# Second cross attention of a two-layer decoder: scores in half bursts, six turned tiles, the output product in four parts

## The chip, the cores and the metric

The kernel runs on one core of one Trainium2 chip. The metric is the device time of one execution in microseconds. Before the change three runs took 2445.8 us in the median (2442.81 to 2445.98).

## The reference, cut to what matters

A decoder of two layers works on x of 8 batches x 128 rows x 512 columns, with a layer norm ahead of each of six blocks. The change lies in the fifth block, the cross attention of layer 1, and in its join to the sixth, a linear layer with 3-bit weights.

```python
def _L1_xattn_ref(queries, keys, values, Wq, Wk, Wv, Wo):
    EMBED, HEADS, GROUP, KV_HEADS, HEAD_DIM = 512, 32, 4, 8, 16
    q = (queries @ Wq).reshape(b, s, KV_HEADS, GROUP, HEAD_DIM)
    k = (keys @ Wk).reshape(b, s, KV_HEADS, HEAD_DIM)
    v = (values @ Wv).reshape(b, s, KV_HEADS, HEAD_DIM)
    scores = jnp.einsum('bqhgd,bkhd->bhgqk', q, k) * scale
    attn = jax.nn.softmax(scores, axis=-1)
    out = jnp.einsum('bhgqk,bkhd->bqhgd', attn, v).reshape(b, s, EMBED)
    return out @ Wo
x = x + _L1_xattn_ref(_layernorm(x, axis=-1), ctx_4096, ctx_4096, ...)
x = x + _L1_ffn_ref(_layernorm(x, axis=-1), ...)
```

## The kernel before

Everything lies in SBUF; weights come in through five slots. Each weight and activation of the large products is split into a high and a low part, and a product is three matmuls (mm3, L552 to L554). Every engine has its own list of instructions, written out by hand, and semaphores alone join them. The first four blocks fill the first 2200 us; they, and the first layer norm in halves, are not touched.

**The attention of the change.** There are 16 steps n, two for each batch b = n // 2 (its part is n % 2). A step has four groups g of 128 x 512 scores. In a step each group goes through this chain:

- TensorE, `scores(n)` (L991): 8 matmuls on strips of 32 rows of the array, group g on strip g, into the four banks sc0, sc1, pj0 and pj1. One burst fills all four.
- VectorE, `row_max(n, g)` (L2001): the negative row maximum.
- ScalarE, `exps(n, g)` (L1352): four Exp into the tile `probs` of the group, of which there is one for each g.
- VectorE, `row_sums(n, g)` (L2008, L2011): the sum and its reciprocal.
- GpSimd, `normalise(n, g)` (L524): probs times the reciprocal, in place.
- TensorE, `transposes(n, g)` (L1005): four turnings into the bank tp or ou1, in turn.
- ScalarE, `turned_out(n, g)` (L1361): the copy to the tile `turned_whole` (four tiles, one for each g).
- TensorE, `values(n)` (L1019): when all four tiles are there, probs times values into the bank pv.

After a batch's second step ScalarE and VectorE copy pv out as a high and a low part, `heads(b)` (L1367, L2017); TensorE then does `output(b)`, the product with Wo, 12 matmuls into the bank ou0 (L552 to L554); VectorE adds it to x and takes the statistics, `add(b)` (L1429, L2023). The queries of the second half of the batches, `queries(1, c)` for c = 0 to 3 (12 matmuls each into ou0, copied out by ScalarE at L1344), have the place of the first half's queries in `act_whole`, so they wait until steps 5 to 7, when those are used up. VectorE also puts three parts of `dequantise` (L1546 to L1550, the 3-bit weights of the next block) into steps 0, 1 and 3. GpSimd's `block_keys` and `pad_values` (L506, L517) prepare keys and values two steps ahead.

Below, M stands for row_max, E for exps, S for row_sums, N for normalise, T for transposes, U for turned_out, V for values, O for output; "step n" is the pass n of TensorE's loop, "odd" and "even" go by n. In that loop (L1066) TensorE does T(n,0), T(n,1), all of scores(n+1), T(n,2), T(n,3), then in even steps the whole O, then V(n). After step 15 come `turned_weights`, the turned rows of the last layer norm, O(7) and the last block's `product`.

Of the kernel before, what the change touches and what calls it, by code (L numbers as in the profile page):

```python
# [17 lines left out]
FP32 = mybir.dt.float32  # L18
# [7 lines left out]
P = 128  # L26
# [62 lines left out]
KG = 4  # L89
NG = B * KVH // KG  # L90


# [19 lines left out]
def build(nc, a):  # L112
    ctx = ExitStack()
    with ctx:
# [33 lines left out]
        with ExitStack() as shared:  # L148
            TW = shared.enter_context(nc.sbuf_tensor("turned_whole", [P, KG, 512], FP32))
        AL = sb("act_lo", [P, NA], F32R)  # L150
# [397 lines left out]
        def _(pe):  # L548
# [410 lines left out]
            def queries(hf, c):  # L959

                n = hf * KC + c
                bank = ou[0] if hf else query_banks[c]
                if n == 0:
                    pe.wait_ge(x_done, OU["l1x"])
                if n == 2:
                    pe.wait_ge(kr_out, 3)
                if n == 3:
                    pe.wait_ge(q_out, 1)
                if n in (4, 5):
                    pe.wait_ge(x_done, OU["l1x"] + n - 2)  # L970
                if n in (6, 7):
                    pe.wait_ge(q_out, n)
                for k in range(KC):
                    w = both(W, lambda t: wpair(t, WQ_SLOTS, k, 512)[:, c * P:(c + 1) * P])
                    last = mm3(bank[:], w, wide(XT, hf)(k), k == 0, k == KC - 1)
                last.then_inc(q_full, 1)

            def scores(n):

                b, part = n // 2, n % 2  # L980
                pe.wait_ge(kx_ready, n + 1)
                pe.wait_ge(q_out, b // HB * KC + 2 * part + 2)
                if n:
                    pe.wait_ge(lx_exp, n * KG)
                else:
                    pe.wait_ge(pj_done, PJ["ln4"] + B)
                for h in range(2):
                    for g in range(KG):
                        r = slice(32 * g, 32 * g + 32)
                        at = (2 * part + h) * HALF + b % HB * S  # L990
                        last = pe.matmul(score_banks[g][:, h * 256:(h + 1) * 256], AF[r, at:at + S], KX[r, n % 2, :],  # L991
                                         start=True, stop=True)
                        if h:
                            last.then_inc(gs_full, 1)
# [13 lines left out]
            def values(n):  # L1008
# [8 lines left out]
                for g in range(KG):  # L1017
                    at = part * P + 32 * g
                    last = pe.matmul(pv[32 * g:32 * g + 32, :], pads(b)[:, at:at + 32], TW[:, g, :],  # L1019
                                     start=part == 0, stop=part == 1)  # L1020
                last.then_inc(pg_full, 1)

            def output(b):
                pe.wait_ge(on_done, b + 1)
                pe.wait_ge(x_done, OU["l1x"] + b)
                pe.wait_ge(q_out, 4 if b < 2 else 5 if b == 2 else 8)
                if b == 0:
                    ready(4, SLOT["l1x"][4])
                    ready(3, SLOT["l1x_o"])
                for c in range(KC):  # L1030
                    last = mm3(ou[0][:], both(A, lambda t: t[:, ON1 + c * P:ON1 + (c + 1) * P]),
                               wrows(WO_SLOTS)(c), c == 0, c == KC - 1)
                last.then_inc(ou_full, 1)

# [28 lines left out]
            turn(4, range(HB + 2, B))  # L1063
            scores(0)
            queries(0, 3)
            for n in range(NG):  # L1066
# [17 lines left out]
            output(B - 1)  # L1084
            for b in range(B):
# [6 lines left out]
        def _(act):  # L1092
# [244 lines left out]
            def queries(hf, c):  # L1337

                n = hf * KC + c
                act.wait_ge(q_full, n + 1)  # L1340
                if hf:
                    act.wait_ge(gs_full, (7 + c // 2) * KG)
                bank = ou[0] if hf else query_banks[c]
                act.activation(AF[:, c * HALF:(c + 1) * HALF], bank[:], ACT.Copy, scale=HD ** -0.5).then_inc(q_out, 1)  # L1344

# [10 lines left out]
            def turned_out(n, g):  # L1356
                t = n * KG + g
                act.wait_ge(tn_full, t + 1)
                if n:
                    act.wait_ge(pg_full, n)  # L1360
                act.activation(TW[:, g, :], turn_banks[t % 2][:], ACT.Copy).then_inc(tn_out, 1)  # L1361

# [14 lines left out]
            for g in range(1, KG):  # L1377
                exps(0, g)
            for n in range(NG - 1):
# [12 lines left out]
                if n == 6:  # L1392
                    queries(1, 1)
                if n == 7:
                    queries(1, 2)
                    queries(1, 3)
            turned_out(NG - 1, 0)
# [20 lines left out]
        def _(dve):  # L1418
# [607 lines left out]
            for g in range(KG):  # L2026
                row_max(0, g)
            for g in range(KG):
                row_sums(0, g)
            dve.wait_ge(w_hi[3], SLOT["l1x_o"] + 1)  # L2030
            dve.tensor_tensor(WL[:, 3, :], RAW[:, 3, :], f32(WH[:, 3, :]), ALU.subtract).then_inc(w_ready[3], 1)
            for n in range(NG - 1):
                for g in range(KG):
# [7 lines left out]
                if n + 2 == NG:  # L2041
                    half_deviation(5, 0)
                row_sums(n + 1, 2)
                if n % 2:
                    heads(n // 2)
                row_sums(n + 1, 3)
            def weights_lo(c):
# [140 lines left out]
```

## Time and profile before

| what | value |
|---|---|
| median of three runs | 2445.8 us (2442.81 to 2445.98) |
| the profiled execution | 2446.34 us |
| its span | 2444.4 us |
| granted TensorE clock, mean of the span | 0.985 |
| TensorE (PE) busy | 2359.7 us, 97% |
| VectorE (DVE) busy | 1253.6 us, 51% |
| ScalarE (ACT) busy | 903.7 us, 37% |
| GpSimd (POOL) busy | 664.5 us, 27% |

The span runs from the first to the last instruction; 1.9 us lie around it. Times in rows are microseconds from the span's start. A clock of 1.00 is 2.4 GHz, 0.50 is 1.2 GHz; a mean between is a stretch that has both.

### The profile page before, as it was taken

To read this page: it belongs to the slowest core of one execution; us is meant where nothing else is said; L and a number is where in the kernel's file an instruction comes from. 1 tells how busy PE (TensorE), PEld (TensorE's weight loads), DVE (VectorE), ACT (ScalarE), POOL (GpSimd) and SP (SyncE) were. 2 spreads that over 40 slices of the span, in tenths; PEclk is the share of its full clock that TensorE was granted. 3 is DMA by queue.
4 is the path that set the end of the run, shared out by engine and by line. 5 is a ranking of instruction groups with operands and counts; after the bars stand their busy time and mean duration, and the time that the engine had idled before them with its cause. 6 is when DMAs were issued, how large, how long until landed. Compare 5 with 4: busy or idle time off the path is not lost.

```text
span 2444.4 us, 38460 instructions
## 1 busy us (share of the span) xinstructions
PE 2359.7 (97%) x13227; PEld 2014.3 (82%) x13227; DVE 1253.6 (51%) x2924; ACT 903.7 (37%) x2234; POOL 664.5 (27%) x381
## 2 busy tenths in 40 slices
PE   6999899999999999998999999999999999998788
PEld 5788698888888888887888888888888888886455
DVE  6444644444444444456654444444444444457766
ACT  2111344444444444443233333333333333334764
POOL 3444423222222322231321111111111111112542
PEclk9999999999999999999999999999999999999889
DMA  3210212111111211211111111111111111110000
GB/s 118 78 43 26 95 53 85 52 51 69 51 51 61 76 51 51 69 52 35 40 51 45 45 45 45 45 45 43 38 37 34 39 43 45 45 54 1 1 1 35
DMA packets 36831, 118.96 MB, mean 49 GB/s; under 512 B 4904, under 2 KB 7336, under 8 KB 36784
## 3 DMA queue, kind: packets, MB, share of 16 engines
q1 hardware_dynamic: 36784, 118.35, 14.0%
q8 instruction: 28, 0.46, 0.1%
q14 instruction: 19, 0.16, 0.0%
HBM read 116.24 MB, written 2.10 MB: 48 GB/s over the span
## 4 chain that ended last, share of the span: by engine, by line
PE 90%; DVE 5%; POOL 2%; ACT 1%; issue 1%; DMA 0%; POOLq 0%; ACTq 0%; SPq 0%; DVEq 0%
PE pj L552 19%; PE pj L553 19%; PE pj L554 19%; PE ou L552 7%; PE ou L554 6%; PE ou L553 6%; PE pv L742 2%; PE sc L879 2%; PE pv L888 2%; PE sc L726 2%; PE tp L733 1%; POOL w_lo L418 1%; PE sc L991 1%; DVE neg_max L2001 1%; POOL w_hi L416 1%
## 5 line engine op out<-in xcount | busy, mean ns | idle before, releaser
L410 POOL TENSOR_TENSOR w_lo<-raw,w_hi 128x1024 fp32r<-128x1024 f32 x145 | 346.7, 2391 | 1438.1 <-ACT w_hi L1126 1398.6
L552 PE MATMUL pj<-xt_hi,w_hi 128*128 128x512 f32 x1232 | 499.7, 406 | 6.2 <-DVE w_lo L1581 2.5
L553 PE MATMUL pj<-xt_lo,w_hi 128*128 128x512 f32 x1232 | 483.1, 392 | 0.0
L554 PE MATMUL pj<-xt_hi,w_lo 128*128 128x512 f32 x1232 | 482.4, 392 | 0.0
L552 PE MATMUL ou<-w_hi,act_hi 128*128 128x512 f32 x684 | 275.3, 402 | 0.8 <-DVE x L1429 0.6
L552 PEld LDWEIGHTS pj<-xt_hi,w_hi 128*128 128x128 f32 x1232 | 233.4, 189 | 50.3 <-DVE w_lo L1581 2.9
L554 PEld LDWEIGHTS pj<-xt_hi,w_lo 128*128 128x128 f32 x1232 | 232.6, 189 | 49.6
L554 PE MATMUL ou<-w_hi,act_lo 128*128 128x512 f32 x684 | 268.1, 392 | 0.0
L553 PE MATMUL ou<-w_lo,act_hi 128*128 128x512 f32 x684 | 267.6, 391 | 0.0
L553 PEld LDWEIGHTS pj<-xt_lo,w_hi 128*128 128x128 f32 x1232 | 233.7, 190 | 41.2
L1429 DVE TENSOR_TENSOR x<-x,ou 128x512 f32<-128x512 f32 x192 | 130.8, 684 | 244.6 <-PE ou L554 244.2
L1287 ACT ACTIVATE side<-pj 128x512 f32<-128x512 f32 (+1 forms) x256 | 125.6, 491 | 341.1 <-PE pj L554 341.1
L1898 DVE TENSOR_TENSOR queries_keys<-side,pj 128x512 f32<-128x512 f32 x128 | 88.1, 688 | 184.5 <-ACT side L1287 184.5
L1202 ACT ACTIVATE queries_keys<-pj 128x512 f32<-128x512 f32 x128 | 76.5, 598 | 243.8 <-PE pj L554 243.8
L552 PE MATMUL pj<-w_hi,xt_hi 128*128 128x256 f32 (+1 forms) x544 | 160.7, 295 | 2.5 <-DVE x_sum L1507 1.6
L1126 ACT ACTIVATE w_hi<-raw 128x1024 fp32r<-128x1024 f32 x146 | 153.5, 1051 | 20.5 <-PE ou L554 18.7
L552 PEld LDWEIGHTS ou<-w_hi,act_hi 128*128 128x128 f32 x684 | 129.2, 189 | 36.8 <-issue 10.8
L553 PE MATMUL pj<-w_lo,xt_hi 128*128 128x256 f32 (+1 forms) x544 | 157.4, 289 | 0.0
L554 PE MATMUL pj<-w_hi,xt_lo 128*128 128x256 f32 (+1 forms) x544 | 157.4, 289 | 0.0
L554 PEld LDWEIGHTS ou<-w_hi,act_lo 128*128 128x128 f32 x684 | 129.1, 189 | 27.9
L553 PEld LDWEIGHTS ou<-w_lo,act_hi 128*128 128x128 f32 x684 | 129.4, 189 | 24.5
L552 PE MATMUL pj<-w_hi,ctx_hi 128*128 128x256 f32 x512 | 147.8, 289 | 0.7 <-POOL w_lo L418 0.7
(241 smaller groups left out, 4533.2 us busy)
## 6 DMA issues: line engine op xcount, KB each, us to landing
raw<-in_l1a_w SPq DMA_DIRECT2D x80, 512.0 KB, 4.1
raw<-in_l0x_w SPq DMA_DIRECT2D x64, 512.0 KB, 4.2
side<-in_side SPq DMA_DIRECT2D x32, 512.0 KB, 3.9
raw<-in_ffn_w SPq DMA_DIRECT2D x15, 512.0 KB, 3.3
raw<-in_l0f_w SPq DMA_DIRECT2D x6, 512.0 KB, 3.7
raw<-in_l1x_w SPq DMA_DIRECT2D x6, 512.0 KB, 3.7
raw<-in_taylor_w SPq DMA_DIRECT2D x5, 512.0 KB, 7.3
x<-in_x SPq DMA_DIRECT2D x2, 1024.0 KB, 7.4
```

The source lines that it names most:

```text
L410: pool.tensor_tensor(WL[:, s, :], RAW[:, s, :], f32(WH[:, s, :]), ALU.subtract).then_inc(w_ready[s], 1)
L552: pe.matmul(out, wh, xh, start=first, stop=False)
L553: pe.matmul(out, wh, xl, start=False, stop=False)
L554: return pe.matmul(out, wl, xh, start=False, stop=last)
L726: last = pe.matmul(score(j)[:, h * S:(h + 1) * S], heads_of(0, h, j), heads_of(1, h, j), start=True, stop=True)
L742: last = pe.matmul(pv[:, h * S:(h + 1) * S], VT[:, n, h * S:(h + 1) * S], TA[:, n % 2, h * S:(h + 1) * S], start=True, stop=True)
L879: last = pe.matmul(score(j)[:, h * S:(h + 1) * S], heads_of(1, h, j), heads_of(0, h, j), start=True, stop=True)
L1126: act.activation(WH[:, s, :], RAW[:, s, :], ACT.Copy).then_inc(w_hi[s], 1)
L1202: act.activation(QK[:, n, :], bank[:], ACT.Copy, scale=S ** -0.5 if n < 2 else 1.0).then_inc(pj_done, 1)
L1287: act.activation(F[:, x % 2, 0:w], pj[bank][:, 0:w], ACT.Sigmoid).then_inc(la_sg, 1)
L1429: dve.tensor_tensor(dst, dst, ou[bank][:], ALU.add).then_inc(x_done, 1)
L1898: dve.tensor_tensor(dst, F[:, x % 2, 0:w], pj[bank][:, 0:w], ALU.mult).then_inc(pj_done, 1)
```

## The change

It moves the order of the four engines' work in the attention's steps and changes three buffers. In all it leaves the arithmetic as it was.

- `scores` is issued in two halves of two groups, (0, 1) and (2, 3). The first half of step n+1 stands ahead of T(n,0) and waits for E(n,1) only; the second follows T(n,1) and waits for E(n,3).
- `turned_whole` has six tiles, used round by round, so that V(n-1) can stand in step n, behind T(n,0).
- O(b) is cut into its four parts (three matmuls each): the first at the end of even step 2b+2, the others in odd step 2b+3, ahead of T(n,1), ahead of T(n,2) and ahead of T(n,3).
- The queries of the second half go to free room in `raw` (QUERIES), so queries(1,0) is done before the loop, (1,1) and (1,2) after steps 0 and 1, and (1,3) in step 4.
- ScalarE takes E(n+1,g) ahead of U(n,g), one by one. VectorE takes M(n+1,0), M(n+1,1), then S(n,2), S(n,3), then M(n+1,2), M(n+1,3), S(n+1,0), S(n+1,1). `heads(b)` moves from step 2b+1 to step 2b+2 and `add(b)` from an even step to the odd step behind it; add(6) falls behind the loop.

```diff
+NTW = 6
...
-            TW = shared.enter_context(nc.sbuf_tensor("turned_whole", [P, KG, 512], FP32))
+            TW = shared.enter_context(nc.sbuf_tensor("turned_whole", [P, NTW, 512], FP32))
...
+        RAWF = RAW[:, 0:2, :].rearrange("p s n -> p (s n)")
+        QUERIES = [AF, RAWF]
...
-            def scores(n):
+            def scores(n, two):
...
-                pe.wait_ge(kx_ready, n + 1)
-                pe.wait_ge(q_out, b // HB * KC + 2 * part + 2)
+                if two == 0:
+                    pe.wait_ge(kx_ready, n + 1)
+                    pe.wait_ge(q_out, b // HB * KC + 2 * part + 2)
                 if n:
-                    pe.wait_ge(lx_exp, n * KG)
-                else:
+                    pe.wait_ge(lx_exp, (n - 1) * KG + 2 * two + 2)
+                elif two:
                     pe.wait_ge(pj_done, PJ["ln4"] + B)
                 for h in range(2):
-                    for g in range(KG):
+                    for g in (2 * two, 2 * two + 1):
...
             for n in range(NG):
+                late = n % 2 and n > 1
+                if n + 1 < NG:
+                    scores(n + 1, 0)
                 transposes(n, 0)
+                if n:
+                    values(n - 1)
+                if late:
+                    output(n // 2 - 1, (1,))
                 transposes(n, 1)
+                if n == 4:
+                    queries(1, 3)
                 if n + 1 < NG:
-                    scores(n + 1)
+                    scores(n + 1, 1)
+                if late:
+                    output(n // 2 - 1, (2,))
                 transposes(n, 2)
+                if late:
+                    output(n // 2 - 1, (3,))
                 transposes(n, 3)
                 if n % 2 == 0 and n:
-                    output(n // 2 - 1)
-                if n + 1 == NG:
-                    turned_weights(0)
-                    turned_weights(1)
-                values(n)
-                for c in {5: (0,), 6: (1,), 7: (2, 3)}.get(n, ()):
-                    queries(1, c)
+                    output(n // 2 - 1, (0,))
+                if n in (0, 1):
+                    queries(1, n + 1)
+            turned_weights(0)
+            turned_weights(1)
+            values(NG - 1)
...
             for n in range(NG - 1):
+                exps(n + 1, 0)
                 turned_out(n, 0)
+                if n in (1, 2):
+                    queries(1, n)
+                exps(n + 1, 1)
                 turned_out(n, 1)
-                if n == 6:
-                    queries(1, 0)
+                if n % 2 == 0 and n:
+                    heads(n // 2 - 1)
+                exps(n + 1, 2)
                 turned_out(n, 2)
-                exps(n + 1, 0)
-                exps(n + 1, 1)
+                if n == 4:
+                    queries(1, 3)
+                exps(n + 1, 3)
                 turned_out(n, 3)
-                exps(n + 1, 2)
-                if n % 2:
-                    heads(n // 2)
-                exps(n + 1, 3)
...
             for n in range(NG - 1):
-                for g in range(KG):
-                    row_max(n + 1, g)
+                row_max(n + 1, 0)
+                row_max(n + 1, 1)
+                row_sums(n, 2)
+                row_sums(n, 3)
+                row_max(n + 1, 2)
+                if n % 2 == 0 and n:
+                    heads(n // 2 - 1)
+                row_max(n + 1, 3)
                 if n in (0, 1, 3):
                     dequantise((0, 1, 3).index(n) + 1)
                 row_sums(n + 1, 0)
                 row_sums(n + 1, 1)
-                if n % 2 == 0 and n:
+                if n % 2 and n > 1:
                     add(n // 2 - 1)
...
+            half_deviation(5, 0)
+            row_sums(NG - 1, 2)
+            row_sums(NG - 1, 3)
+            add(B - 2)
```

TensorE, a step of the loop before the change (in the second half of the attention). tp and ou are the turnings' banks, sc and pj the scores' banks, pv takes the values:

```order
L1005 MATMUL tp<-identity,probs 128x128 x4
L1005 MATMUL ou<-identity,probs 128x128 x4
L991 MATMUL sc<-keys_blocked,act_whole 128x256 x2
L991 MATMUL pj<-keys_blocked,act_whole 128x256 x2
L991 MATMUL sc<-keys_blocked,act_whole 128x256 x2
L991 MATMUL pj<-keys_blocked,act_whole 128x256 x2
L1005 MATMUL tp<-identity,probs 128x128 x4
L1005 MATMUL ou<-identity,probs 128x128 x4
```

TensorE, an odd step after the change, to its third turning:

```order
L996 MATMUL sc<-keys_blocked,raw 128x256 x4
L1010 MATMUL tp<-identity,probs 128x128 x4
L1024 MATMUL pv<-turned_whole,values_padded 32x512 x4
L556 MATMUL ou<-w_hi,act_hi 128x512
L557 MATMUL ou<-w_lo,act_hi 128x512
L558 MATMUL ou<-w_hi,act_lo 128x512
L1010 MATMUL ou<-identity,probs 128x128 x4
L996 MATMUL pj<-keys_blocked,raw 128x256 x4
L556 MATMUL ou<-w_hi,act_hi 128x512
L557 MATMUL ou<-w_lo,act_hi 128x512
L558 MATMUL ou<-w_hi,act_lo 128x512
L1010 MATMUL tp<-identity,probs 128x128 x4
```

The one burst of four groups has become two of two groups each, the values of the step before stand behind the first turning, and parts of the output stand between turnings.

VectorE, an even step before the change (the maxima of one step, its sums, and add between them):

```order
L2001 TENSOR_REDUCE neg_max<-sc 128x4 x2
L2001 TENSOR_REDUCE neg_max<-pj 128x4 x2
L2008 TENSOR_REDUCE row_sums<-probs 128x4
L2011 RECIPROCAL row_recip<-row_sums 128x4
L2008 TENSOR_REDUCE row_sums<-probs 128x4
L2011 RECIPROCAL row_recip<-row_sums 128x4
L1429 TENSOR_TENSOR x<-x,ou 128x512
L2023 BN_STATS bn_stats<-x 128x6
L2008 TENSOR_REDUCE row_sums<-probs 128x4
L2011 RECIPROCAL row_recip<-row_sums 128x4
```

VectorE, an even step after the change:

```order
L2018 TENSOR_REDUCE neg_max<-sc 128x4 x2
L2025 TENSOR_REDUCE row_sums<-probs 128x4
L2028 RECIPROCAL row_recip<-row_sums 128x4
L2025 TENSOR_REDUCE row_sums<-probs 128x4
L2028 RECIPROCAL row_recip<-row_sums 128x4
L2018 TENSOR_REDUCE neg_max<-pj 128x4
L2034 TENSOR_TENSOR act_lo<-pv,act_hi 128x512
L2018 TENSOR_REDUCE neg_max<-pj 128x4
L2025 TENSOR_REDUCE row_sums<-probs 128x4
L2028 RECIPROCAL row_recip<-row_sums 128x4
```

The sums of groups 2 and 3 of the step before now stand between the maxima of groups 1 and 2, and heads (act_lo) stands ahead of the last maximum.

## Rows read from the trace of the kernel before

**Rows 1.** Stretches: length; busy PE, PEld, DVE, ACT, POOL; granted clock; DMA share, GB/s.
```profile
2254.00:2408.00 154.00, 123.74 (x780) 77.77 (x772) 113.91 (x233) 109.84 (x336) 78.01 (x92) 0.83 0.00 1
...
2312.00:2316.00 4.00, 2.31 (x14) 1.26 (x15) 3.03 (x8) 3.85 (x14) 2.40 (x3) 1.00 0.00 0
...
2372.00:2376.00 4.00, 1.76 (x11) 0.26 (x9) 2.97 (x7) 3.52 (x13) 2.18 (x3) 0.69 0.00 0
```
**Rows 2.** Waits from 2254 to 2405: us in total, times, longest.
```profile
PE pv L1019 <- ACT turned_whole L1361: 19.2, 8, 2.8
```
**Rows 3.** VectorE in order of time: first maxima of steps 1, 6, 9, 11, 13, 15.
```profile
2264.44 1.29 DVE L2001 TENSOR_REDUCE neg_max<-sc 128x4 f32<-128x512 f32 x2 [1.09 <-PE pj L991]
...
2309.54 1.29 DVE L2001 TENSOR_REDUCE neg_max<-sc 128x4 f32<-128x512 f32 x2
...
2345.80 1.29 DVE L2001 TENSOR_REDUCE neg_max<-sc 128x4 f32<-128x512 f32 x2 [7.93 <-PE pj L991]
...
2363.04 1.29 DVE L2001 TENSOR_REDUCE neg_max<-sc 128x4 f32<-128x512 f32 x2 [1.31 <-PE pj L991]
...
2380.41 1.29 DVE L2001 TENSOR_REDUCE neg_max<-sc 128x4 f32<-128x512 f32 x2 [1.31 <-PE pj L991]
...
2397.61 1.29 DVE L2001 TENSOR_REDUCE neg_max<-sc 128x4 f32<-128x512 f32 x2 [1.27 <-PE pj L991]
```
**Rows 4.** VectorE from 2381: maxima, add (two instructions), two sums; then heads(7).
```profile
2381.62 1.28 DVE L2001 TENSOR_REDUCE neg_max<-pj 128x4 f32<-128x512 f32 x2
...
2384.54 0.66 DVE L1429 TENSOR_TENSOR x<-x,ou 128x512 f32<-128x512 f32 x1
...
2385.84 0.67 DVE L2008 TENSOR_REDUCE row_sums<-probs 128x4 f32<-128x512 f32 x1
...
2386.64 0.66 DVE L2008 TENSOR_REDUCE row_sums<-probs 128x4 f32<-128x512 f32 x1
...
2409.78 0.69 DVE L2017 TENSOR_TENSOR act_lo<-pv,act_hi 128x512 fp32r<-128x512 f32 x1
```
**Rows 5.** ScalarE from 2381, in order of time; GpSimd from 2386.
```profile
2381.52 2.17 ACT L1352 ACTIVATE probs<-sc,neg_max 128x128 f32<-128x128 f32 x8
2383.52 0.66 ACT L1361 ACTIVATE turned_whole<-ou 128x512 f32<-128x512 f32 x1
2383.99 2.24 ACT L1352 ACTIVATE probs<-pj,neg_max 128x128 f32<-128x128 f32 x8
...
2386.80 2.04 POOL L524 TENSOR_TENSOR probs<-probs,row_recip 128x512 f32<-128x512 f32 x2 [0.98 <-DVE row_recip L2011]
```
**Rows 6.** TensorE at 2.4 GHz: turning, score burst, turning; values, queries, turning.
```profile
2317.97 0.60 PE L1005 MATMUL ou<-identity,probs 128*128 128x128 f32 x4
2318.50 0.48 PE L991 MATMUL sc<-keys_blocked,act_whole 32*128 32x256 f32 x2
2318.51 0.48 PE L991 MATMUL pj<-keys_blocked,act_whole 32*128 32x256 f32 x2
...
2319.58 0.66 PE L1005 MATMUL tp<-identity,probs 128*128 128x128 f32 x4
...
2323.47 1.06 PE L1019 MATMUL pv<-turned_whole,values_padded 128*32 128x512 f32 x8
2324.49 0.50 PE L552 MATMUL ou<-xt_hi,w_hi 128*128 128x512 f32 x1
...
2327.39 0.60 PE L1005 MATMUL tp<-identity,probs 128*128 128x128 f32 x4
```
**Rows 7.** TensorE at 1.2 GHz: values behind a wait, turnings, score burst; next turning.
```profile
2374.54 1.94 PE L1019 MATMUL pv<-turned_whole,values_padded 128*32 128x512 f32 x8 [2.24 <-ACT turned_whole L1361]
2376.41 1.12 PE L1005 MATMUL tp<-identity,probs 128*128 128x128 f32 x4
...
2378.31 0.80 PE L991 MATMUL sc<-keys_blocked,act_whole 32*128 32x256 f32 x2
...
2380.33 0.66 PE L1005 MATMUL tp<-identity,probs 128*128 128x128 f32 x4
```

More of the change, by code:

```diff
@@ L968, in queries @@
                     pe.wait_ge(q_out, 1)
-                if n in (4, 5):
-                    pe.wait_ge(x_done, OU["l1x"] + n - 2)
-                if n in (6, 7):
+                if n in (4, 5, 6):
                     pe.wait_ge(q_out, n)
+                if n == 7:
+                    pe.wait_ge(x_done, OU["l1x"] + 1)
                 for k in range(KC):
@@ L976, in queries @@
                 last.then_inc(q_full, 1)
-            def scores(n):
+            def scores(n, two):
                 b, part = n // 2, n % 2
-                pe.wait_ge(kx_ready, n + 1)
-                pe.wait_ge(q_out, b // HB * KC + 2 * part + 2)
+                if two == 0:
+                    pe.wait_ge(kx_ready, n + 1)
+                    pe.wait_ge(q_out, b // HB * KC + 2 * part + 2)
                 if n:
-                    pe.wait_ge(lx_exp, n * KG)
-                else:
+                    pe.wait_ge(lx_exp, (n - 1) * KG + 2 * two + 2)
+                elif two:
                     pe.wait_ge(pj_done, PJ["ln4"] + B)
                 for h in range(2):
-                    for g in range(KG):
+                    for g in (2 * two, 2 * two + 1):
                         r = slice(32 * g, 32 * g + 32)
                         at = (2 * part + h) * HALF + b % HB * S
-                        last = pe.matmul(score_banks[g][:, h * 256:(h + 1) * 256], AF[r, at:at + S], KX[r, n % 2, :],
-                                         start=True, stop=True)
+                        last = pe.matmul(score_banks[g][:, h * 256:(h + 1) * 256], QUERIES[b // HB][r, at:at + S],
+                                         KX[r, n % 2, :], start=True, stop=True)
                         if h:
@@ L1018, in values, with output @@
                     at = part * P + 32 * g
-                    last = pe.matmul(pv[32 * g:32 * g + 32, :], pads(b)[:, at:at + 32], TW[:, g, :],
+                    last = pe.matmul(pv[32 * g:32 * g + 32, :], pads(b)[:, at:at + 32], TW[:, (n * KG + g) % NTW, :],
                                      start=part == 0, stop=part == 1)
                 last.then_inc(pg_full, 1)
[L1023 to L1030, printed above, removed]
+            def output(b, chunks):
+                if chunks[0] == 0:
+                    pe.wait_ge(on_done, b + 1)
+                    pe.wait_ge(x_done, OU["l1x"] + b)
+                    pe.wait_ge(q_out, 8 if b else 7)
+                    if b == 0:
+                        ready(4, SLOT["l1x"][4])
+                        ready(3, SLOT["l1x_o"])
+                for c in chunks:
                     last = mm3(ou[0][:], both(A, lambda t: t[:, ON1 + c * P:ON1 + (c + 1) * P]),
                                wrows(WO_SLOTS)(c), c == 0, c == KC - 1)
-                last.then_inc(ou_full, 1)
+                if chunks[-1] == KC - 1:
+                    last.then_inc(ou_full, 1)
             def product(b):
@@ L1083, in _ @@
             turn(5, range(2))
-            output(B - 1)
+            output(B - 1, range(KC))
             for b in range(B):
@@ L2027, in _ @@
                 row_max(0, g)
-            for g in range(KG):
-                row_sums(0, g)
+            row_sums(0, 0)
+            row_sums(0, 1)
             dve.wait_ge(w_hi[3], SLOT["l1x_o"] + 1)
@@ L2032, in _ @@
             for n in range(NG - 1):
-                for g in range(KG):
-                    row_max(n + 1, g)
+                row_max(n + 1, 0)
[6 more added lines that the diff above has]
+                row_max(n + 1, 3)
                 if n in (0, 1, 3):
```

26 lines of the change are left out of this document (8 added, 18 removed).

## The prediction, made before the change was run

> **What bounds the kernel now.** The page's slices show TensorE busy nearly everywhere until 2254, and no line that the change touches lies there. So I read only the 154 us from 2254 to 2408, first as a stretch: TensorE busy 123.7, VectorE 113.9, ScalarE 109.8, GpSimd 78.0, and a granted clock of 0.83, which is a third of the time at 1.2 GHz [rows 1]. No engine is full; the steps are a relay. The waits say where it is handed on: TensorE's values wait for the fourth turned tile, 19.2 us in all [rows 2], and VectorE's first maximum of a step waits for the score burst [rows 3]. The order of time shows the beat. From the first maximum of step 1 to that of step 15 are 2397.61 - 2264.44 = 133.2 us for 14 steps. Steps 1 to 6 take 45.1, a late pair (11 to 13) 17.4, and the step into 9 alone has 7.93 of waiting, because two query products stand in it behind each other with their copies between [rows 3]. The late pair's odd burst runs at 1.2 GHz, after a wait of 2.24 [rows 7].
>
> **Prices.** From the distance between starts, all at 2.4 GHz. TensorE: a turning T 0.5 (2317.97 to 2318.50) and 0.66 to its result; the burst of four groups 1.08 (2318.50 to 2319.58); values V 1.02; 12 matmuls of a product 2.90 with what surrounds them, so 0.78 for a part of three, an estimate of 3 x 0.23 and the change of operands [rows 6]. VectorE: M 0.6 (two in 1.21), S 0.8, add 1.30, heads 0.6 to 0.69 [rows 3, 4]. ScalarE: E 1.0 (eight Exp in 2.00) with a result after 1.2, U 0.47 [rows 5]. GpSimd: N 1.0 [rows 5]. A handover costs 0.05 to 0.1.
>
> **The score halves.** In the burst, sc and pj start 0.01 apart: the four strips of the array work side by side [rows 6]. A half uses only two strips. Its price is between 0.54 (it costs by the number of matmuls) and 1.08 (by the number of rounds); I take 1.08, since what starts together in the row must then start in as many rounds as before. The two halves so cost TensorE 1.08 a step more, 16 us in all, which is on the path only where TensorE is. The upper end is above 1.08 by what a change of the array's shape costs. The burst's first start to the next turning has that in it, once each way. The Trainium skill ("TensorEngine Tiling (Array Packing)", Key Properties) says that a change of tiling mode drains TensorE, which speaks against this change: it makes two bursts of one and puts the values between turnings. The row agrees in kind: the burst's first matmuls take 0.48 where a turning's start came 0.53 before [rows 6].
>
> **Each engine's load for a pair of steps.** TensorE: four half bursts 4.3, eight T 4.0, two V 2.0, four parts of the output 3.1, sum 13.4. VectorE: eight M 4.8, eight S 6.4, add 1.3, heads 0.6, sum 13.1. ScalarE: eight E 8.0, eight U 3.8, heads 0.5, sum 12.3. GpSimd: 8 and some 1.7 for keys and values. So 13.4 is the floor, against 17.4 now.
>
> **The cycle of a pair.** The floor isn't reached, since the engines wait for each other in an order. I followed each through its new order. The cycle that closes: T(n,0) 0.5, V 1.0, O part 0.8, T(n,1) 0.5, the second half burst with its result 1.15 (4.0 so far), M and M 1.2, S and S 1.6, add 1.3, M(n+2,0) 0.7, then on ScalarE E, U, E, U 3.0 and heads 0.6, on VectorE heads 0.6, M 0.6, S 0.9, on GpSimd N 1.05 (handovers 0.05 in most), back to T: 15.6 for a pair. Of the odd step 8.5, of the even 7.1. Queued behind the new waits: heads on VectorE waits about 0.7 for ScalarE's heads, with M(n+1,3) and both S behind it; that is in the cycle. The wait that goes (V for the fourth tile) is covered, because V(n-1) now starts behind T(n,0), when U(n-1,3) is 0.4 or less away. The six tiles hold nobody up: U(n,2) waits for V(n-1), which is done about 3 us earlier. GpSimd has over 4 us of air in a pair, and the keys and pads for which TensorE waits keep their lead of two steps.
>
> **Steps 1 to 6.** They get the four query products (2.8 each, three of them here, one ahead of step 1), which leave steps 5 to 7. Following the order: 8.7 and 8.6 for the first two (S(n,2) and S(n,3) behind two M, then N, T, 2.8 for queries and the half burst), 7.7, then 10.2 (dequantise 1.8 and add on VectorE in one step), 9.9 (queries(1,3) between T(4,1) and the second half). Sum 45.1, as now. Clock gained back, products taken in.
>
> **Steps 6 to 15.** Now 2397.61 - 2309.54 = 88.1 [rows 3]. After: five odd and four even intervals, 42.5 + 28.4 = 70.9. Gain 17.2, of which some 9 is the product work that went to the front and its waits.
>
> **Before step 1.** M(1,0) loses S(0,2) and S(0,3) ahead of it (1.6) and its wait of 1.09 [rows 3]; TensorE has queries(1,0) and a half burst first. I take a gain of 2.2 of the possible 2.7; at worst it is 0, if the queries' copies are late.
>
> **Behind step 15.** Here it costs. From M(15,0) to the start of VectorE's heads(7) are 2409.78 - 2397.61 = 12.2 now [rows 3, 4]. After, S(14,2) and S(14,3) stand in there (1.6), TensorE has V(14) and three parts of O(6) between its turnings (3.4), and add(6) with 1.3 waits for them ahead of the layer norm's rows and heads(7). Followed through: 16.2, so 4.0 lost. The rest runs as now.
>
> **Sum.** -17.2 - 2.2 + 4.0 = -15.4. Against the profiled execution's 2446.34 (span 2444.4 and 1.9 around it) that is 2430.9; the median shown is 0.5 below that execution, so I say 2430.4. Bounds: a half burst of 0.54 takes 0.5 from a pair, 2.5 in all; handovers of 0.05 or 0.1, some twenty in a pair, give 1 a pair either way, 5 in all; the front 0 to 2.7. The case's own range is 2424 to 2437.
>
> **Rivals.**
>
> *The load alone counts* (the order has more air than I find): pairs at 13.4 to 14.5, nine intervals in 60 to 65, net -21 to -28, so 2418 to 2425, say 2422. For it: VectorE and ScalarE are both near the load. Against: heads, add and the S pairs stand in fixed places. Chance 0.12.
>
> *Only the queries' place helps*: the steps stay at the pace of now, because half bursts and the four parts put on TensorE's path what the earlier start takes off. Nine intervals at the pace without queries, 4.5 pairs of 17.4, are 78; gain 10, net with front and tail -8, so 2438. For it: the two half bursts, and turned tiles that VectorE's order delays. Against: in the pair of now the waits of 2.24 and 1.3 lie open [rows 3, 7]. Chance 0.14.
>
> *The clock*, the rival on the other side. At 1.2 GHz a pair's work is, by the rows, T 0.95 (1.9 for two), V 1.87, the burst 2.02 [rows 7], so the halves 8.1, turnings 7.6, values 3.7 and the output, twice 2.7, 5.4: 24.8 against 15.6, all of it TensorE's own. Some 116 us of steps at full clock become longer by 9.2/15.6 of the share f that is spent low: 68 f. It eats the 15.4 at f = 0.23, and now f is 0.34 [rows 1]; then the time is 2446 + 8 = 2454. What speaks for it: the change makes TensorE wait shortly and often, and costs it more when slow. Against it: the four microseconds from 2312 stayed at 1.00 with TensorE busy 2.31 of 4, and the clock was lower where 1.76 of 4 were busy, at an idle time of 2.24 [rows 1, 7]; in my cycle TensorE is busy 13.4 of 15.6 and no wait is over 0.7. The Trainium skill ("TensorE: Matmul & The Clock Gate", A second HAM failure mode: psum-queue depth-cycling) says that frequent short idle times between matmul groups can make the clock swing between its levels; by that this rival would hold. The trace shows falls only at longer waits. Chance 0.09.
>
> *It doesn't do what it says*: a wait that is more than its comment, such as E(n+1,0) ahead of U(n,0) holding V(n-1) back so that the early values wait as before. U(n-1,3) is the last of ScalarE's step and V(n-1) comes after T(n,0); if it is late by 1.5 in each step, 14 steps give back 21 and the time is about 2450; at 1 each it is no change. Chance 0.05. The main case has 0.60.
>
> **Chances.** 0.2% is 4.9 us, about what a measurement of this kernel can tell from no change. Faster by more: the main case, the load case, most of the second rival: 0.85. Within: 0.07, its edge and the last rival. Slower: 0.08, the clock and a bit. The range 2420 to 2442 leaves out half of the load case's far end and the two on the other side.
>
> **What would show it.** M(15,0) less M(1,0) at 116 (113 to 122); a late pair of 15 to 16 with the odd step longer; granted clock over 0.95 from 2254 to the attention's end; score halves of 1.0 to 1.1; TensorE's wait for turned_whole under 6 us in all; heads(7) some 16 behind M(15,0). Wrong, if the clock of that stretch is under 0.9, if halves take over 1.3, or if the waits of V stay over 15 us.

## The result, and the profile after

| | before | after |
|---|---|---|
| median, least and most of six runs each | 2445.89 us (2442.81 to 2446.93) | 2435.55 us (2432.68 to 2438.97) |
| the profiled execution, its span | 2446.34, 2444.4 | 2432.68, 2430.8 |
| M(1,0) to M(15,0) | 133.2 | 117.6 |
| M(15,0) to heads(7) on VectorE | 12.2 | 17.7 |

The ratio is 0.996 with a 95% interval of 0.9947 to 0.9973: faster by 10.3 us. The forecast was 2430.4, with a range of 2420 to 2442.

The stretches of [rows 1], in the profile of after (length; busy PE, PEld, DVE, ACT, POOL; granted clock; DMA share, GB/s):

```profile
2254.00:2408.00 154.00, 134.87 (x833) 85.45 (x832) 122.71 (x255) 114.41 (x345) 78.75 (x92) 0.99 0.00 1
...
2372.00:2376.00 4.00, 4.00 (x29) 2.60 (x22) 2.25 (x6) 2.91 (x10) 2.61 (x3) 1.00 0.02 4
```

The granted clock rose from 0.83 to 0.99. Waits of after from 2252 to 2399 (in total, times, longest): the first answers to [rows 2], the second to the waits in [rows 3].

```profile
PE pv L1024 <- ACT turned_whole L1380: 2.6, 5, 0.5
...
DVE neg_max L2018 <- PE pj L996: 14.4, 14, 2.4
```

TensorE's wait for the turned tile fell from 19.2 to 2.6. First maxima of steps 1, 6, 11, 12, 13 and 15 of after, as [rows 3]:

```profile
2261.50 1.29 DVE L2018 TENSOR_REDUCE neg_max<-sc 128x4 f32<-128x512 f32 x2 [1.08 <-PE sc L996]
...
2307.62 1.29 DVE L2018 TENSOR_REDUCE neg_max<-sc 128x4 f32<-128x512 f32 x2 [1.53 <-PE sc L996]
...
2347.38 1.27 DVE L2018 TENSOR_REDUCE neg_max<-sc 128x4 f32<-128x512 f32 x2
...
2354.59 1.29 DVE L2018 TENSOR_REDUCE neg_max<-sc 128x4 f32<-128x512 f32 x2
...
2363.23 1.27 DVE L2018 TENSOR_REDUCE neg_max<-sc 128x4 f32<-128x512 f32 x2
...
2379.09 1.27 DVE L2018 TENSOR_REDUCE neg_max<-sc 128x4 f32<-128x512 f32 x2
```

A late pair (from the first maximum of step 11 to that of step 13) takes 2363.23 - 2347.38 = 15.85, of which 7.2 are the even interval (11 to 12) and 8.6 the odd one (12 to 13). TensorE in a late odd step:

```profile
2339.21 0.66 PE L1010 MATMUL tp<-identity,probs 128*128 128x128 f32 x4 [0.49 <-POOL probs L528]
2339.79 1.06 PE L1024 MATMUL pv<-turned_whole,values_padded 128*32 128x512 f32 x8
2340.79 0.50 PE L556 MATMUL ou<-w_hi,act_hi 128*128 128x512 f32 x1
...
2341.59 0.60 PE L1010 MATMUL ou<-identity,probs 128*128 128x128 f32 x4
2342.12 1.13 PE L996 MATMUL pj<-keys_blocked,raw 32*128 32x256 f32 x8
2343.18 0.50 PE L556 MATMUL ou<-w_hi,act_hi 128*128 128x512 f32 x1
```

From start to start these are T 0.58, V 1.00, a part of the output 0.80, T 0.53 and the half burst 1.06. The tail of after, TensorE, ScalarE and VectorE in order of time:

```profile
2386.77 1.07 PE L1010 MATMUL tp<-identity,probs 128*128 128x128 f32 x4 [1.56 <-POOL probs L528]
...
2387.76 1.94 PE L1024 MATMUL pv<-turned_whole,values_padded 128*32 128x512 f32 x8
...
2391.97 1.28 ACT L1130 ACT_TABLE_LOAD   x1
...
2393.19 0.69 DVE L1446 TENSOR_TENSOR x<-x,ou 128x512 f32<-128x512 f32 x1 [3.87 <-PE ou L558]
...
2396.83 0.69 DVE L2034 TENSOR_TENSOR act_lo<-pv,act_hi 128x512 fp32r<-128x512 f32 x1
```

From the start of the first part of dequantise, the last work that the change leaves as it was, the whole difference can be added up: to M(1,0) 9.01 where 11.25 were, steps -15.6, tail +5.6, behind it 33.9 where 34.6 were, and ahead of it -0.7. That is the -13.6 between the two spans. The place of that dequantise scatters between 2251.0 and 2256.4 over the kernels of this study, which share the work ahead of it, so the -0.7 says nothing of the change, and below kernels are compared by M(1,0) to M(15,0) ("the steps") and M(15,0) to heads(7) ("the tail").

### The profile page after: what moved, and what is told of

The parts are those of the page before. It is cut to its first block, busy times and chain, and to the rows that moved or that the text cites. A ratio compares the mean times of both kernels' runs of the same rounds, so it can differ in the third digit from the quotient of the medians.

```text
span 2430.8 us, 38454 instructions
## 1 busy us (share of the span) xinstructions
PE 2359.2 (97%) x13227; PEld 2013.1 (83%) x13227; DVE 1257.8 (52%) x2924; ACT 904.3 (37%) x2234; POOL 666.2 (27%) x381
## 4 chain that ended last, share of the span: by engine, by line
PE 90%; DVE 5%; POOL 2%; ACT 2%; issue 1%; DMA 0%; POOLq 0%; SPq 0%; ACTq 0%; DVEq 0%
PE pj L556 19%; PE pj L557 19%; PE pj L558 19%; PE ou L556 7%; PE ou L558 6%; PE ou L557 6%; PE pv L746 2%; PE sc L883 2%; PE pv L892 2%; PE sc L730 2%; PE tp L737 1%; POOL w_lo L422 1%; DVE neg_max L2018 1%; POOL w_hi L420 1%; ACT probs L1371 1%
## 5 line engine op out<-in xcount | busy, mean ns | idle before, releaser
L1147 ACT ACTIVATE w_hi<-raw 128x1024 fp32r<-128x1024 f32 x146 | 153.6, 1052 | 20.5 <-PE ou L558 18.7
```

Of the source, the lines that this page charges most:

```text
L1147: act.activation(WH[:, s, :], RAW[:, s, :], ACT.Copy).then_inc(w_hi[s], 1)
```

## The experiments

The theory was that of the prediction (the relay of the four engines, and the clock that it keeps). Its main rival was "only the queries' place helps". Runs 1 and 2 add one thing to the kernel before, runs 3 to 5 and 7 to 10 edit the changed kernel, run 6 joins runs 1 and 2, and run 11 repeats the changed kernel. "After" is the changed kernel in its first profile. Each ratio is to runs of the kernel before, taken beside it.

**1. Before, with the queries' new place alone.**

```diff
+        QUERIES = [AF, RAWF]
...
+            queries(1, 0)
...
-                for c in {5: (0,), 6: (1,), 7: (2, 3)}.get(n, ()):
+                for c in {0: (1,), 1: (2,), 3: (3,)}.get(n, ()):
```

> The kernel before, with one part of the change alone: the second half's queries go to free room in raw and are made before the loop, after steps 0, 1 and 3. Theory R (the relay: most of the gain is the new order of the steps): from the first maximum of step 6 to that of step 15 the 88.1 us become about 79 (five odd steps of 10.0, four even of 7.2), the steps before become up to 8 us longer, and the whole gains 1 to 6 us. Rival Q (only the queries' place helps): it gains as much as the change, 10 us or more.

Measured 2435.14 us, ratio 0.9952 (0.9936 to 0.9969): as much as the whole change, where the theory had allowed 1 to 6 us. The steps took 122.5, the tail 13.7, and the step starts lie 11.3, 11.3, 7.2, 11.7, 7.2 apart for steps 1 to 6 (before 10.3, 10.3, 7.2, 10.1, 7.2), then 9.1, 7.3, 9.1 to step 9 (before 10.1, 9.9, 16.3). Three products cost 3.6 in steps 1 to 6, and their absence gives 10.8 in steps 6 to 9 and 3.6 behind. Its stretch from 2254 to 2400, its waits for the turned tile in it, and two of them in late steps:

```profile
2254.00:2400.00 146.00, 118.14 (x800) 75.92 (x792) 116.39 (x236) 112.21 (x340) 78.10 (x92) 0.91 0.00 1
```
```profile
PE pv L1022 <- ACT turned_whole L1363: 18.3, 8, 2.8
```
```profile
2365.38 1.07 PE L1022 MATMUL pv<-turned_whole,values_padded 128*32 128x512 f32 x8 [2.25 <-ACT turned_whole L1363]
...
2381.02 1.94 PE L1022 MATMUL pv<-turned_whole,values_padded 128*32 128x512 f32 x8 [2.25 <-ACT turned_whole L1363]
```

All eight waits are still there (18.3 us, before 19.2), at a clock of 0.91 (0.82 before in the same window). Behind the first of the two shown TensorE kept 2.4 GHz, and that odd interval took 8.2, less than the 8.6 of after; behind the second it fell to 1.2 GHz, and the interval took 9.1. So the wait that the early values remove costs little beside TensorE's clock.

**2. Before, with eight matmuls into the free bank ou0 ahead of V in odd steps.** Nobody reads what they compute; they are work added to keep TensorE busy.

```diff
+            def filler(n):
...
+                for k in range(8):
+                    pe.matmul(ou[0][:], wpair(WH, WQ_SLOTS, k % KC, 512)[:, 0:P], wide(XT, 0)(0)[0], start=True, stop=True)
...
+                elif n % 2:
+                    filler(n)
```

> The kernel before, with eight matmuls more in each odd step 1 to 13, whose results nobody reads (bank ou0), in TensorE's wait ahead of the values. They do 1.7 us at 2.4 GHz in a wait of 2.2. Theory C (the gain of the change is the clock, which the change keeps up because TensorE waits for shorter times): the stretch from 2254 to 2408 is granted over 0.95, odd steps fall from 10.0 to 7.3 to 7.8 us, and the whole gains 12 to 18 us, as much as the change or more. Theory R (the order of the waits sets the pace and the clock goes along): the gain is under 5 us.

Measured 2436.32 us, ratio 0.9963 (0.9951 to 0.9976), a gain of 9.7: less than the 12 to 18 of the clock theory, and twice what the other theory allowed. The steps took 124.2 and the late odd ones 8.2 where before has 10.0:

```profile
2364.35 2.09 PE L1027 MATMUL ou<-xt_hi,w_hi 128*128 128x512 f32 x8
2366.83 1.06 PE L1019 MATMUL pv<-turned_whole,values_padded 128*32 128x512 f32 x8 [0.39 <-ACT turned_whole L1369]
```

V now runs at 2.4 GHz (1.06, against 1.94 in [rows 7]). The late pair took 15.6, a little less than the changed kernel's 15.8: in the late steps the old order lacked only the clock.

**3. The change, with one burst of four groups behind T(n,1).**

```diff
-                if n + 1 < NG:
-                    scores(n + 1, 0)
...
-                    scores(n + 1, 1)
+                    scores(n + 1)
```

> The changed kernel, with the scores in one burst of four groups again, at the place of the second half (behind T(n,1)); all else as changed. Theory R: the first maxima now wait for T(n,0), V(n-1), a part of the output and T(n,1), so the sums of groups 2 and 3 stand behind them and a pair of steps takes 18 to 20 us instead of 15.8; 15 to 28 us slower than the changed kernel. Rival H (a half burst costs 1.06 like a whole one, so halving mostly adds TensorE work): a pair falls to 15 or less and the whole is 3 to 6 us faster than the changed kernel.

Measured 2490.47 us, ratio 1.0179 (1.0162 to 1.0196), 55 us above the changed kernel, with a late pair of 23.9: far more than the 15 to 28 us and the 18 to 20 that I had expected. TensorE issues the burst in one go and then waits for the next probs:

```profile
2411.17 0.48 PE L995 MATMUL sc<-keys_blocked,raw 32*128 32x256 f32 x2
...
2415.60 1.12 PE L1009 MATMUL tp<-identity,probs 128*128 128x128 f32 x4 [3.29 <-POOL probs L528]
```
```profile
PE tp L1009 <- POOL probs L528: 20.2, 11, 3.3
```

(The second is of 2360 to 2420.) VectorE's order, with S(n,2) and S(n,3) between maxima, presumes scores that arrive in halves. So the new order needs its half bursts, which cost 1.06 each as priced; that halves beat one burst in the old order is not shown.

**4. The change with its tail in another order:** the table for sqrt loaded ahead of U(15,1), add(6) behind the turned rows.

```diff
+            half_deviation(5, 0)
             turned_out(NG - 1, 1)
-            half_deviation(5, 0)
...
-            add(B - 2)
...
+            dve.wait_ge(tn_full, (NG - 1) * KG + 2)
...
+            add(B - 2)
```

> The changed kernel with another end: ScalarE's square root for the last layer norm ahead of U(15,1) instead of behind it, and add(6) behind the first two turned rows on VectorE instead of ahead of them. If VectorE's queue behind add(6) sets the end, as the trace shows (add(6) waits 3.9 us, then VectorE is full for 4.3 us), heads(7) comes 1.0 to 1.4 us sooner and the whole gains about 1 us, within the noise of the whole time but plain in the trace. If the end is set by TensorE's list (V(14) and three parts of O(6) between turnings), nothing moves.

Measured 2433.45 us, ratio 0.9944 (0.9927 to 0.9961); the tail took 15.5, 2.3 less, where I had expected 1.0 to 1.4. But TensorE's V(14), behind the same wait of 1.55, here ran at 2.4 GHz, and that is not the order's doing alone: run 7 parts the two. In its profile steps 4 to 7 took 12.0, 11.2, 10.3 (after 10.4, 10.2, 8.1), at a lower clock; run 11 returns to this.

**5. The same, and steps 3 and 4 mended.** In the profile of after two waits stand there: T(4,0) waits for its probs, which I put down to dequantise and add in one step on VectorE, and O(1) for ScalarE's copy of queries(1,3).

```profile
2296.54 0.65 PE L1010 MATMUL tp<-identity,probs 128*128 128x128 f32 x4 [1.57 <-POOL probs L528]
...
2305.60 0.47 PE L556 MATMUL ou<-w_hi,act_hi 128*128 128x512 f32 x1 [2.00 <-ACT raw L1363]
```

```diff
+                if n == 4:
+                    queries(1, 3)
                 exps(n + 1, 2)
                 turned_out(n, 2)
-                if n == 4:
-                    queries(1, 3)
...
+                if n == 3:
+                    dequantise(3)
                 row_max(n + 1, 2)
```

> The changed kernel with three mends: the other end of e4_tail, ScalarE's copy of queries(1,3) ahead of E(5,2) instead of behind U(4,2), and the last part of dequantise in VectorE's wait of 1.7 us of step 3 instead of behind its last maximum. Theory L (local holes): TensorE's waits of 2.0 us ahead of O(1) in step 4 and of 1.6 us ahead of T(4,0) go, and with them the place at which the clock fell in e4_tail; from the first maximum of step 4 to that of step 6, 20.6 us in the changed kernel and 23.2 in e4_tail, become 16 to 18, the whole gains 3 to 5 us over the changed kernel and its runs spread less. Rival (the holes are covered by slack): the stretch stays over 20 us and the whole within 2 us.

Measured 2432.66 us, ratio 0.9943 (0.9927 to 0.996). Steps 4 to 6 took 18.7 (after 20.7; I had expected 16 to 18), the steps 116.1, the tail 15.5, and the clock of the stretch was 1.00. The second wait went, but the first shrank only to 1.11, so dequantise was a part of its cause:

```profile
2299.74 0.66 PE L1010 MATMUL tp<-identity,probs 128*128 128x128 f32 x4 [1.11 <-POOL probs L528]
```

**6. Runs 1 and 2 together**, the old order with the queries early and the filler.

> The kernel before, with the early queries of e1_queries_early and the filler matmuls of e2_filled in each odd step 1 to 13. If the two gains (11 and 10 us) are of different causes, query products in the wrong place and a falling clock, they add where they do not overlap: a pair of steps at 15.4 to 15.7 us throughout, from the first maximum of step 1 to that of step 15 114 to 118 us, the whole 2425 to 2430, some 7 us faster than the changed kernel although its steps are in the old order. If they are one cause (each only keeps TensorE busier, so the clock up), the sum is 2433 to 2436, like either.

Measured **2427.69 us** (2427.28 to 2428.25), ratio 0.9926 (0.9909 to 0.9942), faster than both kernels. The steps took 116.2, the tail 12.4. Run 1 took 10.7 from the steps and run 2 9.0; together they took 17.0 of the possible 19.7. A late pair took 15.6. No half burst, no sixth tile and no cut output is in it.

```profile
2254.00:2400.00 146.00, 127.74 (x889) 85.01 (x890) 121.89 (x251) 114.62 (x345) 78.00 (x92) 0.99 0.00 1
```

**7. The change with four turned tiles.**

```diff
-NTW = 6
+NTW = 4
```

> The changed kernel with four turned tiles in place of six; all else as it is. Theory (the early values free the tiles long before the next copy wants one): in the profile V(n-1) is done about 3 us ahead of U(n,2), and with four tiles U(n,0) waits for V(n-1), which in the changed kernel starts 0.5 after T(n,0), as U(n,0) itself does. So each U(n,0) is held by up to 0.5 to 1.0 us a step, 0 of it on the path if E(n+1,1) behind it has air, up to 15 us in all if not. If the six tiles were for nothing: M(1) to M(15) at 117 to 118, a late pair at 15.8, within 1 us of the changed kernel. If they carry the change: a late pair at 16.8 to 17.8, M(1) to M(15) at 124 to 132, 2442 to 2450. I expect the first within 3 us: U(n,0) can't start before T(n,0) is done, V needs 1.0 more, and ScalarE has 1.3 to 1.7 of air in a step.

Measured 2438.07 us in nine runs, ratio 0.9967 (0.9957 to 0.9977), against 2435.78 for the changed kernel itself beside it (run 11); the intervals overlap. A late pair took 15.85, as with six. ScalarE waited for V twice in all of 2254 to 2400:

```profile
ACT turned_whole L1380 <- PE pv L1024: 2.8, 2, 2.0
```

One is near step 6, the other (2.03) in the tail, where it holds nothing up: the copy behind it waits again, 0.65 for T(15,1). The tail took 16.2, 1.6 less than that of after, though the order is the same. The difference is TensorE's clock: behind a wait of 1.54 (after 1.56) for T(15,0) it stayed at 2.4 GHz:

```profile
2394.09 0.66 PE L1010 MATMUL tp<-identity,probs 128*128 128x128 f32 x4 [1.54 <-POOL probs L528]
2394.68 1.07 PE L1024 MATMUL pv<-turned_whole,values_padded 128*32 128x512 f32 x8
```

So the fall in the tail of after costs 1.6, and against the 16.2 the other order of run 4 is worth 0.7. The two added tiles hold nobody up and free nobody in a late pair; whether they are worth the 2.3 us between the medians stays open, since steps 4 to 7 (10.4, 12.8, 10.2) again had low clock.

**8. The change with O whole at the end of the even step.**

```diff
-                if late:
-                    output(n // 2 - 1, (1,))
...
-                    output(n // 2 - 1, (0,))
+                    output(n // 2 - 1, range(KC))
```

> The changed kernel with the output product whole again, at the end of the even step (12 matmuls behind T(n,3)). Theory R by its cycle: the odd step loses 0.8 us (one part that stood ahead of the second half burst), the even step gains 2.1 us of TensorE in a row ahead of the next first half burst, so a pair takes 16.5 to 17.2 instead of 15.8, and the whole is 4 to 8 us slower; the end gets back about 2 us, since O(6) no longer stands between the turnings of step 15. Rival: the place of the parts does not matter, a pair stays at 15.8.

Measured 2443.16 us in ten runs, ratio 0.9982 (0.9973 to 0.9992). A late pair took 16.5 (the last one 18.2, since the clock fell in it), and the step from 5 to 6 15.4 where after has 10.2:

```profile
2311.48 0.76 PE L556 MATMUL ou<-w_hi,act_hi 128*128 128x512 f32 x1 [1.99 <-ACT raw L1357]
...
2315.85 1.13 PE L996 MATMUL sc<-keys_blocked,act_whole 32*128 32x256 f32 x8
```

The same late copy of queries(1,3) now holds the whole product, in part at 1.2 GHz, ahead of the next scores: 4.4 from the one to the other, where a part takes 0.9. In the tail, which kept 2.4 GHz, it took 15.1: 2.6 less than after, but only 1.1 less than run 7 at the same clock. The cut is worth 0.7 a pair and most of the loss in step 5, and costs some 1.1 in the tail.

**9. The change with VectorE's heads behind M(n+1,3).**

```diff
                 row_max(n + 1, 2)
+                row_max(n + 1, 3)
                 if n % 2 == 0 and n:
                     heads(n // 2 - 1)
-                row_max(n + 1, 3)
```

> The changed kernel with VectorE's heads behind the last maximum of the even step instead of ahead of it. Theory R: VectorE's wait of 0.46 for ScalarE's heads lies in the cycle and is now filled by that maximum, so the even step is 0.3 to 0.6 us shorter and a pair takes 15.3 to 15.5; the whole gains 1.5 to 3.5 us. Rival (TensorE's list is the cycle): a pair stays at 15.8 or grows by up to 0.6, since the first part of the output then starts later.

Measured 2431.34 us, ratio 0.9945 (0.9928 to 0.9962). A late pair took 15.3, the steps 115.0, the tail 15.6. VectorE ran both maxima at once and then heads without a wait, where after has 0.46:

```profile
2368.28 1.29 DVE L2018 TENSOR_REDUCE neg_max<-pj 128x4 f32<-128x512 f32 x2 [0.38 <-PE pj L996]
2369.48 0.68 DVE L2034 TENSOR_TENSOR act_lo<-pv,act_hi 128x512 fp32r<-128x512 f32 x1
```

So heads' wait was in the cycle, as the prediction put it; the gain shows in the odd interval (8.1 for 8.6), not in the even one where I had looked for it. The tail is shorter mostly by the clock, which did not fall here (16.2 in run 7).

**10. All repairs together:** runs 5 and 9, and O(6) whole at the end of step 14.

```diff
-                late = n % 2 and n > 1
+                late = n % 2 and 1 < n < NG - 1
...
-                    output(n // 2 - 1, (0,))
+                    output(n // 2 - 1, (0,) if n < NG - 2 else range(KC))
```

> The changed kernel with all single repairs together: VectorE's heads behind M(n+1,3), the table load for sqrt and add(6) moved in the tail, O(6) whole at the end of step 14, ScalarE's copy of queries(1,3) ahead of E(5,2), dequantise(3) one place earlier. If the repairs add up: M(1) to M(15) at 113 to 114 (a late pair 15.4), M(15) to heads(7) at 13.5 to 14, together 6 to 7 below the changed kernel, 2427 to 2430, level with the kernel that leaves the old order and only moves the queries and fills the gap. If they do not (the tail takes what the steps give): 2431 to 2433.

Measured **2427.95 us** (2425.14 to 2429.9), ratio 0.9925 (0.9909 to 0.9942): level with run 6, with no added work. All four of its runs lie below all ten of the changed kernel; the interval is clear of the 0.9947 to 0.9973 of the first comparison and just touches the 0.9941 to 0.9974 of the one beside it (run 11). The steps took 114.1 and the tail 14.6 (I had expected 13.5 to 14); all four runs had a mean clock of 0.995 or 0.996.

**11. The changed kernel again.**

> The changed kernel once more, nothing edited, for the spread of what is read from one profile. M(1) to M(15) within 1.5 of 117.6, the odd and even steps from 10 on at 8.6 and 7.2, M(15) to heads(7) at 17.7, or 1 less if TensorE's clock does not fall in the tail. The time 2433 to 2438. If the clock falls at another place than in the first profile, the steps it falls in become longer by 1 to 3 and the rest stays.

Measured 2435.78 us (2432.8 to 2437.61), ratio 0.9957 (0.9941 to 0.9974). The tail (17.8) and the late pairs (15.8) came out as in the first profile, but the steps took 123.6, 6.0 more and 4.5 beyond what I had expected, since the clock fell between step 3 and step 7. Their starts lie 7.7, 12.0, 13.4, 9.4 apart (7.7, 10.4, 10.2, 8.1 in the first profile). TensorE in run 11:

```profile
2282.63 0.63 PE L1010 MATMUL ou<-identity,probs 128*128 128x128 f32 x4 [0.59 <-ACT turned_whole L1380]
2283.75 0.50 PE L556 MATMUL ou<-w_hi,act_hi 128*128 128x512 f32 x1 [0.50 <-DVE act_lo L2034]
...
2286.27 0.89 PE L1010 MATMUL tp<-identity,probs 128*128 128x128 f32 x4 [0.49 <-POOL probs L528]
2287.09 1.94 PE L1024 MATMUL pv<-turned_whole,values_padded 128*32 128x512 f32 x8
...
2296.97 1.12 PE L1010 MATMUL tp<-identity,probs 128*128 128x128 f32 x4 [1.56 <-POOL probs L528]
...
2307.51 0.77 PE L556 MATMUL ou<-w_hi,act_hi 128*128 128x512 f32 x1 [1.99 <-ACT raw L1363]
...
2309.06 2.08 PE L996 MATMUL sc<-keys_blocked,act_whole 32*128 32x256 f32 x8
```

There are three falls: at 2286, behind waits of 0.59, 0.50 and 0.49; at 2297, at the wait for probs; at 2307, at the wait for the copy. The first profile has the same rows up to the first of them, 1.14 later, and the same two waits behind it, and no fall at any of the three.

## Why the prediction was right, and where its numbers were off

The total came out within the range, but the total alone proves little: one buffer moved gives as much (run 1), and the changed kernel's own steps took 117.6 in one profile and 123.6 in the other. What bears the mechanism out are the terms below.

**The steps.** Forecast 116.0, found 117.6. Steps 1 to 6 took 46.1 (forecast 45.1), steps 6 to 15 71.5 (70.9). The pair, its halves of 8.5 and 7.1, and the cycle through heads are confirmed (15.8, of 8.6 and 7.2; run 9). Of the 1.0 in front, 0.6 lies in the two steps with the waits of run 5: I had seen dequantise and add in one step and taken 10.2 for it (10.4), and had sized queries(1,3) at 9.9 (10.25) without O(1) behind its copy. The other 0.4 is the step from 2 to 3 (9.0 for 8.6), which no run looks into.

**The half burst.** 1.08 forecast, 1.06 found: with two strips in place of four it costs as much as a full burst, by its rounds and not by its matmuls. From T to the half took 0.53, from T to V 0.58 and from V on 1.00 (before 1.02), where T was priced at 0.5. The drain at a change of tiling mode, which the Trainium skill names ("TensorEngine Tiling (Array Packing)", Key Properties), adds at most 0.1 at a change in these rows.

**Before step 1.** -2.2 forecast, -2.2 found.

**The tail.** +4.0 forecast, +5.6 found, and the term that was off is the clock, which the sum took to be full. TensorE waits 1.56 for T(15,0) and in both profiles of the changed kernel then fell to 1.2 GHz (V(14) took 1.94, at full clock 1.07). In run 7, where it did not fall, the same order took 16.2, the forecast's very number. At full clock, reordering gives 0.7 of the 4.0 back (15.5, run 4), and together with runs 5 and 9 and O(6) whole 1.6 (14.6, run 10).

**The sum.** -15.4 forecast against the profiled execution, -13.6 found between the spans: 1.6 short in the steps, 1.6 in the tail, and 1.4 given back outside, of which the forecast had nothing (0.7 ahead, 0.7 behind). That this profile comes within 1.8 of the forecast is in part luck: the 0.7 ahead lies in the scatter of work that the change leaves alone, and this was the fastest of its six executions. The median lies 2.9 above it, 5.1 above the forecast. One cause is the clock, which in most runs seems to fall somewhere: the nine other runs of the unedited kernel had a mean clock of 0.992 to 0.996 (0.996 in the first profile), and one of 0.993 shows 6.0 lost in steps 4 to 7. How much of the 2.9 it is, beside the scatter ahead of the attention, is not shown.

**The rivals.** *Only the queries' place helps* was priced at 2438 with a chance of 0.14, and is the strongest reading of the whole: that part alone gives 10.9 (run 1). Its pricing erred in taking the pace of now as fixed: the late pairs kept 17.4 in my sum and took 15.4 to 16.5 in run 1, since the clock rose from 0.82 to 0.91, though the eight waits for the turned tile stayed. Its reason was half wrong too: the other parts do speed the steps, by 4.9 in the first profile (122.5 to 117.6) and not at all in the second (123.6), and the tail takes 4.1 back (13.7 to 17.7). *The load alone counts* is out: 15.8 is no 13.4. (Its far end was also added up wrongly: 60 for the nine intervals, with the front and the tail as in the sum, nets -26 and not -28.) *The clock* came true in part. Its price was near: in run 11 the steps had a clock of 0.94, a share of 0.12 at 1.2 GHz, for which the price says 8, and 6.0 were lost. I had written that the trace shows falls only at longer waits; run 11 shows one behind waits of 0.6 and less. And that no wait is over 0.7 held in the late pairs alone: steps 3 and 4 and the tail have 1.57, 2.00 and 1.56. It cost 6 of the gain and not all of it, because the late pairs kept 1.00 in both profiles of the changed kernel. *It doesn't do what it says* is out: 2.6 of waiting for the turned tile.

**What would show it** held but for heads(7) at 17.7 for 16, and in run 11 the steps, 123.6 for at most 122, and the stretch's clock (2254 to 2400), 0.94 for 0.95.

Three things stay open: why the old order with the queries early keeps the clock in some odd steps (8.2) and not in others (9.1) at the same wait of 2.25; what decides in which execution of the changed kernel it falls; and what the new order gives without the queries' new place, or with the filler, neither of which was run.

## What to carry to other kernels

Where an engine's clock falls at a wait, fill the wait before removing it: eight unread matmuls in a gap told in one run what the gap cost (9.7 us), and beside them a new order of four engines could be judged for itself (a pair of 15.8, against 15.6 for the old one at full clock). Take a change of many parts apart before believing in the largest: here moving one buffer gave as much as the whole, and the reordering came out ahead of it, by 7.2, only once its steps and its tail were mended (run 10), and then level with the old order and its filler. A step's work that is spread over the next one must be paid once at the end; price that tail at both clocks, since its first wait may cost the full one (16.2 or 17.7 here).

## What the hardware showed that I had not expected

The same instructions with the same waits, 1.14 us apart, ran once at 2.4 GHz throughout and once with three falls to 1.2 GHz (run 11 against after). Four microseconds of run 11, and of the first profile those of the same work, 1.14 later:

```profile
2284.00:2288.00 4.00, 3.50 (x23) 1.61 (x22) 3.90 (x10) 2.76 (x10) 2.06 (x3) 0.82 0.02 4
```
```profile
2285.14:2289.14 4.00, 3.50 (x24) 1.64 (x24) 3.90 (x10) 2.99 (x11) 2.06 (x3) 1.00 0.02 4
```

TensorE's waits in the 20 us before were 0.59, 0.59, 0.50 and 0.49 in both. The tail shows the same: behind 1.56 and 1.55 it fell in both profiles of the changed kernel, behind 1.54 and 1.55 it did not in runs 7 and 4. So the order alone does not decide it, and one profile does not tell a kernel's clock. The Trainium skill ("TensorE: Matmul & The Clock Gate", A second HAM failure mode: psum-queue depth-cycling) says that short idle times between groups of matmuls, frequent enough, make the clock swing between its levels. Run 11 agrees at 2286; the late pairs, with waits of 0.49, 0.53, 0.34 and 0.25 a pair, do not: there no profile of the changed kernel shows it. Run 8, with the output whole, does show it in its last pair, behind 0.64, 0.34 and 0.21:

```profile
2379.14 0.58 PE L556 MATMUL ou<-w_hi,act_hi 128*128 128x512 f32 x1 [0.21 <-DVE act_lo L2028]
2379.51 0.63 PE L557 MATMUL ou<-w_lo,act_hi 128*128 128x512 f32 x1
```

The mean clock also moved without TensorE waiting less: from 0.82 to 0.91 over 2254 to 2400 in run 1, where its waits add up to 29.2 us (27.7 before). That run only took products out of the late steps and put them into the early ones.
